# Second cross-attention of a decoder block: order of the matrix products in a window, place of the output projection, and the layout of its sums

## The chip, the cores and the metric
The kernel runs on one core of one Trainium2 chip. The metric is the time of one launch on the device, in microseconds (us). Three runs of the kernel before took 2831.57, 2815.93 and 2821.0 us; the median is 2821.0 us.

## What is computed
Six stages run one after the other on a tensor x of 4 batches x 512 tokens x 256 channels: attention, cross-attention and experts of layer 0, then linear attention, cross-attention and experts of layer 1. After each stage the result is added to x and normalised. The change is in the fifth stage and in the beginning of the sixth. The fifth computes

```
v = einsum('nlhd,ed->nlhe', context, Wv)      # 1024 context tokens, 16 heads of 16 channels
k = einsum('nlhd,ed->nlhe', context, Wk)
q = einsum('nlhd,ed->nlhe', x, Wq)            # 512 tokens of x
energy = einsum('nqhd,nkhd->nhqk', q, k)
attention = softmax(energy / sqrt(256), axis=-1)
out = einsum('nhql,nlhd->nqhd', attention, v).reshape(4, 512, 256)
x = layernorm(x + out @ Wo.T + bo)
```

The sixth sends every token through 16 experts and a shared one.

## The kernel before, in words
The function `l1_cross` (from L992) writes the stage. A unit is one batch with a group of four heads: 4 batches x 4 groups = 16 units, numbered 0 to 15. A unit has 8 windows, numbered 0 to 7, one for each block of 128 context tokens. The lists `between`, `after` and `at` (L1026 to L1039) name what each window does, and the function `side` gives that list to all five engines, each of which writes its own part of it, in that order. Nothing is scheduled afterwards.

In a window TensorE (PE) does the following for the current unit. The score products (`sc`, L1125) of two heads at a time write four banks of PSUM. They come in two halves: half 0 is heads 0 and 1, half 1 is heads 2 and 3. ScalarE (ACT) takes the exponential of a half (L1197). The value products (`pv`, L1110) of the block before follow; they use all 128 rows of the array.

Four more products in a window look ahead to the next unit (`max`, L1143). They are called maximum products 0, 1, 2 and 3 here. Each multiplies 128 queries of one head with 512 keys, and VectorE (DVE) takes the maximum of each row from PSUM (L1247), which the exponential needs later. Their heads are 2, 3, 0 and 1 (`max_of`), so that they stand on other rows of the array than the score products written beside them. After all 32 maxima of a unit, DVE merges them (`mq`, L1252), PE transposes them (`turn`, L1149), ACT copies them (L1217), and the DMA queue of SyncE (SP) writes them as a row under the queries (L1331).

Windows 0 to 4 of an even unit and 0 to 2 of an odd unit also carry a projection for the unit two ahead: `k` twice, `q`, and in even units `v` twice (L1155, L1159, L1166). These are called windows with a projection, the others windows without one. ACT evacuates `k` and `q` in two copies (L1205, L1207).

Maximum products, projections, `turn`, the output projection and transposes of x (`tp`) share three banks of PSUM in turn (`Turns`, `take`). Each may start only when the use three places before it in this ring has been read. The order of the ring in a window with a projection is: maximum products 0 and 1, projection, maximum products 2 and 3.

After the last block of a unit ACT copies the sums to `E` (`ev`, L1222). `E` holds in each group of 32 partitions 16 rows of values and 16 equal rows of the softmax's denominator. SP sends the denominators through DRAM (L1336, L1339), DVE inverts them (`rec`, L1256), SP writes them and reads them back broadcast (L1343, L1347), and GpSimd (POOL) multiplies (`mul`, L1307) into `OT`. `OT` has four slots of 128 partitions for a batch, half of whose rows carry nothing, and the weights `wo` have zeros there. When the four units of a batch are done, the output projection (`wo`, L1173) takes one product for each slot: four for each of the four tiles of 128 tokens. Then x is added (`res`), statistics are taken (`st`), x is scaled (`nr`) and transposed (`tp`). The last batch's output projection is done in the sixth stage (`l1_experts`, L2098).

Of the kernel before, what the change touches and what calls it, by code (L numbers as in the profile page):

```python
# [10 lines left out]
ALU = mybir.AluOpType  # L11
# [45 lines left out]
def program(nc, a, out):  # L57
    with ExitStack() as ctx:
# [89 lines left out]
        def dve_norm(dve, j, b, dst=None):  # L148
            dve.wait_ge(ln["ag"], 4 * j + 4)
            dve.wait_ge(ln["rstd"], j + 1)  # L150
            for i in range(4):
                t = 4 * b + i
                dve.e.tensor_scalar(x[:, t, :] if dst is None else dst(t), x[:, t, :], mv[:, i, 0:1], rstd[:, i:i + 1],
                                    ALU.subtract, ALU.mult).then_inc(ln["nrm"], 1)

# [836 lines left out]
        def l1_cross(c, wy, nx):  # L992
# [8 lines left out]
                                      "row0 row1 den0 den1 dc0 dc1 dr0 dr1 rb0 rb1 gsq gpow gs gtp gT xsq xpow rt lg sig chain")  # L1001
# [7 lines left out]
            R = [sbuf(c, "y_R0", [P, S]), nx["R"]]  # L1009
            OT = [sbuf(c, "y_OT0", [P, 4, S]), nx["OT"]]  # L1010
# [11 lines left out]
            def maxima(t):  # L1022
# [3 lines left out]
            between = {  # L1026
                0: [("pv", 0, 0), ("ev", -1, 0), ("k", 2, 0)],
                1: [("pv", 0, 1), ("k", 2, 1)],
                2: [("pv", 0, 2), ("q", 2, 0)],
                3: [("pv", 0, 3), ("v", 2, 0)],  # L1030
                4: [("pv", 0, 4), ("v", 2, 1)],
                5: [("pv", 0, 5)],
                6: [("pv", 0, 6), ("wo", -1, 0), ("res", -1, 0), ("wo", -1, 1)],
                7: [("pv", 0, 7), ("wo", -1, 2), ("res", -1, 2), ("wo", -1, 3)],
            }
            after = {0: [("st", -2, 0), ("xb", 0, 0)], 1: [("nr", -2, 0)], 2: [("tp", -2, 0)], 3: [("rec", -1, 0)], 4: [("tp", -2, 1)],
                     5: [("turn", 1, 0), ("mul", -1, 0)], 6: [("res", -1, 1)], 7: [("res", -1, 3)]}
            at = {t: [("sc", 0, 0), *maxima(t)[:2], *([("mq", 1, 0)] if t == 5 else []), *[w for w in between[t] if w[0] not in ("pv", "ev")],
                      ("sc", 0, 1), *maxima(t)[2:], *[w for w in between[t] if w[0] in ("pv", "ev")], *after[t]] for t in range(T)}  # L1039
# [8 lines left out]
            def side(u, t):  # L1048
                o = []
                for name, du, i in at[t]:  # L1050
                    v = u + du
                    if name == "pv" and 0 <= u * T + t - 1 < n * T:
                        o.append((name, u, t))
                        continue
                    if name == "sc" and 0 <= u < n and t < T:
                        o.append((name, u * T + t, i))
                        continue
                    once = name == "v" and v % 2 or name in ("pv", "sc")
# [5 lines left out]
                return o + (gate.get(t, []) if u == n - 1 else [])  # L1064
# [28 lines left out]
            def max_of(j):  # L1093

                return j // 8, j // 4 % 2, (2, 3, 0, 1)[j % 4]

# [31 lines left out]
            def pe_prog(pe):  # L1128
                begin(pe)
                for u, t in windows():  # L1130
                    gt = u * T + t
                    for name, v, j in side(u, t):
# [36 lines left out]
                        elif name == "wo":  # L1169
                            bank = take(pe, "wo", v, j)  # L1170
                            pe.wait_ge(s["mul"], v + 1)
                            for kk in range(4):
                                m = pe.e.matmul(bank[:, 0:D], OT[b % 2][:, kk, j * P:(j + 1) * P], wo[:, kk, :],  # L1173
                                                start=kk == 0, stop=kk == 3)
# [15 lines left out]
            def act_prog(act):  # L1190
                begin(act)
                for u, t in windows():
                    for name, v, j in side(u, t):
# [24 lines left out]
                        elif name == "ev":  # L1218
                            act.wait_ge(s["pv"], T * (v + 1))
                            act.wait_ge(s["mul"], v - 1)  # L1220
# [18 lines left out]
            def dve_prog(dve):  # L1239
                begin(dve)  # L1240
                for u, t in windows():
                    for name, v, j in side(u, t):
# [19 lines left out]
                        elif name == "st":  # L1262
                            dve.wait_ge(s["res"], 4 * (b + 1))
                            dve_stats(dve, 20 + b, b)
                        elif name == "nr":
                            dve_norm(dve, 20 + b, b)
# [10 lines left out]
            def pool_prog(pool):  # L1277
# [4 lines left out]
                for u, t in windows():  # L1282
                    for name, v, j in side(u, t):
# [19 lines left out]
                        elif name == "mul":  # L1303
                            pool.wait_ge(s[f"rb{v % 2}"], 16 * 4 * (v // 2 + 1))
                            pool.wait_ge(s["ev"], v + 1)
                            pool.wait_ge(s["ob"], 4 * (v // 4 - 1))
                            pool.e.tensor_tensor(OT[v // 4 % 2][:, v % 4, :], E[v % 2][:], R[v % 2][:], ALU.mult).then_inc(s["mul"], 1)  # L1307
                        elif name == "st":
                            pool_rstd(pool, 20 + v // 4)
                        elif name == "gw":  # L1310
                            pool.wait_ge(g["half"], 1)
                            pool.wait_ge(s["gsq"], 1)
                            pool.e.tensor_tensor(gn[:, 1:2], gn[:, 0:1], ex[0:NE, 1, 0:1], ALU.pow).then_inc(s["gpow"], 1)
                        elif name == "comb":
                            pool_gate(pool, s, 0, 12)

            def sp_prog(sp):
# [5 lines left out]
                for u, t in windows():  # L1323
                    for name, v, j in side(u, t):
# [8 lines left out]
                        elif name == "ev" and v < n - 1:  # L1333
                            sp.wait_ge(s["ev"], v + 1)
                            sp.wait_ge(s[f"dc{v % 2}"], 16 * (v // 2))
                            sp.e.dma_start(yd[v % 2], E[v % 2][16:P:32, :]).then_inc(s[f"den{v % 2}"], 16)  # L1336
                            sp.wait_ge(s[f"den{v % 2}"], 16 * (v // 2 + 1))
                            sp.wait_ge(s[f"dr{v % 2}"], 16 * (v // 2))
                            sp.e.dma_start(C[v % 2][:], yd[v % 2].rearrange("h (a n) -> (h a) n", n=16)).then_inc(s[f"dc{v % 2}"], 16)  # L1339
                        elif name == "rec":  # L1340
# [4 lines left out]
                            sp.wait_ge(s["mul"], v - 1)  # L1345
                            for h in range(4):
                                sp.e.dma_start(R[v % 2][32 * h:32 * h + 32, :], yr[v % 2][h].partition_broadcast(32)).then_inc(s[f"rb{v % 2}"], 16)  # L1347
# [694 lines left out]
        def l1_experts(c, wy, nx):  # L2042
# [8 lines left out]
            s = stage_sems(c, 5, "n", "xsq xpow rt lg sig chain den dc rec dr rb mul ob res wh wl xh xl up g h down acc o")  # L2051
# [12 lines left out]
            def pe_prog(pe):  # L2064
# [13 lines left out]
                for n, (e_, nb) in enumerate(steps):  # L2078
# [13 lines left out]
                    if n == 1:  # L2092
                        pe.wait_ge(s["mul"], 1)
                        for i in range(2):
                            for j in range(2):
                                qt = 2 * i + j
                                for kk in range(4):
                                    r = pe.e.matmul(A[i][:, j * D:(j + 1) * D], OT[:, kk, qt * P:(qt + 1) * P], wo[:, kk, :],  # L2098
                                                    start=kk == 0, stop=kk == 3)
# [97 lines left out]
            def pool_prog(pool):  # L2197
# [10 lines left out]
                pool.e.tensor_tensor(OT[:, 3, :], E[:], R[:], ALU.mult).then_inc(s["mul"], 1)  # L2208
# [7 lines left out]
            def sp_prog(sp):  # L2216
                begin(sp, True)
                sp.e.dma_start(yd[1], E[16:P:32, :]).then_inc(s["den"], 16)
                sp.wait_ge(s["den"], 16)
# [4 lines left out]
                for h in range(4):  # L2224
                    sp.e.dma_start(R[32 * h:32 * h + 32, :], yr[1][h].partition_broadcast(32)).then_inc(s["rb"], 16)
# [28 lines left out]
        with ExitStack() as c1:  # L2254
            wy = {n: sbuf(c1, f"y_{n}", sh) for n, sh in (("wo", [P, 4, D]), ("bo", [P, D]), ("wqk", [P, 2, 2, P]), ("wv", [P, P]), ("part", [P, 1]),
# [12 lines left out]
            for n, sh in (("E", [P, S]), ("C", [P, 16]), ("R", [P, S]), ("OT", [P, 4, S]), ("gw", [NE, D]), ("gn", [NE, 4]), ("gsq", [P, D]),  # L2268
# [43 lines left out]
def layouts(i):  # L2312
# [37 lines left out]
    wo = np.zeros((16, 32, D), np.float32)  # L2350
    wo[:, 0:16, :] = f("L1_xattn_Wo").T.reshape(16, 16, D)
    o["y_wo"] = kt(wo.reshape(512, D))
# [21 lines left out]
```

## Time and profile before

| | us |
|---|---|
| profiled execution, its time | 2816.93 |
| its span, first to last instruction | 2815.0 |
| median of three runs | 2821.0 |
| PE busy | 2569.0 (91% of the span) |
| DVE busy | 1468.7 (52%) |
| ACT busy | 1128.8 (40%) |
| POOL busy | 1086.5 (39%) |

The mean clock granted to TensorE is 0.952 of full speed. Times in rows are microseconds from the start of the span. A busy time is the union of what ran on an engine. `PEld` is the loading of weights, and `SPq` the DMA issues of SyncE. "x2" is the number of instructions merged in a row. `issue` is idle time for which the profile shows no cause. The part in brackets is the engine's idle time ahead of the row and what ended it. The fifth stage runs from about 1960 to 2470 us.

### The profile page before, as it was taken

How to read it: one execution, taken by the hardware profiler on the slowest of the kernel's cores; microseconds unless marked ns; L12 is line 12 of the kernel's file. 1: busy time of each engine (PE TensorE's matmuls, PEld its weight loads, DVE VectorE, ACT ScalarE, POOL GpSimd, SP SyncE). 2: the span in 40 equal slices, each digit the busy share in tenths (PEclk: the TensorE clock that was granted, in tenths of full speed). 3: DMA queues.
4: the chain of work that ended last, by engine and by line, in shares of the span. 5: the costliest groups of instructions: out<-in, count | busy, mean ns of one | idle time of the engine just before them, and what ended most of it. 6: DMA issues, size and time to landing. Idle time of an engine off the chain costs nothing.

```text
span 2815.0 us, 36748 instructions
## 1 busy us (share of the span) xinstructions
PE 2569.0 (91%) x13798; PEld 1529.8 (54%) x13798; DVE 1468.7 (52%) x3205; ACT 1128.8 (40%) x1614; POOL 1086.5 (39%) x735
## 2 busy tenths in 40 slices
PE   5786999999999999997999999687999999889997
PEld 3343556565556555654556665455333333368886
DVE  3444555555555555554433333366677777455455
ACT  3544344444444444442122222132576767631111
POOL 4665466666765676563100000142323323110001
PEclk8997999999999999997899999889799999999999
DMA  2001100000000000003899999510000000000000
GB/s 104 9 9 34 36 12 24 21 19 12 27 18 20 12 12 25 12 1 115 346 372 380 388 386 378 193 39 18 16 22 18 21 17 10 13 16 21 23 23 32
DMA packets 60322, 229.21 MB, mean 81 GB/s; under 512 B 16601, under 2 KB 30577, under 8 KB 44273
## 3 DMA queue, kind: packets, MB, share of 16 engines
q1 hardware_dynamic: 54256, 209.27, 20.2%
q0 software_dynamic: 3584, 9.84, 1.2%
q10 hardware_dynamic: 2304, 7.75, 0.7%
q8 instruction: 110, 1.80, 0.3%
q14 instruction: 68, 0.55, 0.1%
HBM read 216.73 MB, written 9.70 MB: 80 GB/s over the span
## 4 chain that ended last, share of the span: by engine, by line
PE 76%; DVE 9%; issue 4%; DMA 4%; ACT 3%; POOL 3%; SPq 1%; POOLq 0%; ACTq 0%; DVEq 0%
PE PS L680 8%; PE PS L1488 7%; PE PS L663 6%; PE PS L2087 6%; PE PS L711 5%; PE PS L721 4%; PE PS L1506 4%; PE PS L1110 4%; PE PS L2075 4%; PE PS L1125 3%; DMA m_fb<-in_m_fb 3%; PE PS L695 3%; PE PS L1143 3%; DVE y_Mx L1247 2%; PE PS L744 2%
## 5 line engine op out<-in xcount | busy, mean ns | idle before, releaser
L944 POOL TENSOR_TENSOR x_A<-x_A,x_P 128x1024 f32<-128x1024 f32 x190 | 451.4, 2376 | 203.1 <-ACT x_P L791 189.1
L871 DVE CUSTOM_DVE_ANT_0 x_junk<-PS,x_mb 128x512 bf16<-128x512 f32 x512 | 331.0, 685 | 352.2 <-PE PS L695 351.9
L1247 DVE TENSOR_REDUCE y_Mx<-PS 128x1 f32<-128x512 f32 x512 | 324.4, 685 | 126.6 <-PE PS L1143 126.6
L791 ACT ACTIVATE x_P<-PS,x_kb 128x1024 f32<-128x1024 f32 x256 | 271.8, 1112 | 222.8 <-PE PS L667 218.3
L1197 ACT ACTIVATE y_P<-PS 128x1024 f32<-128x1024 f32 x256 | 255.0, 1023 | 113.8 <-PE PS L1125 109.8
L1488 PE MATMUL PS<-m_w,m_xt 128*128 128x512 f32 x624 | 282.8, 596 | 0.6 <-issue 0.6
L680 PE MATMUL PS<-x_P,x_V 128*64 128x512 f32 x1024 | 248.8, 607 | 0.0
L663 PE MATMUL PS<-x_Q,x_K 64*128 64x512 f32 x1536 | 228.4, 400 | 0.0
L1143 PE MATMUL PS<-y_K,y_Q 16*128 16x512 f32 x512 | 188.2, 515 | 32.5 <-DVE y_Mx L1247 28.8
L2087 PE MATMUL PS<-n_xp,n_wp 128*128 128x512 f32 x816 | 211.8, 409 | 4.3 <-POOL n_wp L2203 4.3
L1709 POOL DMA_INDIRECT m_xb<-xd,m_idxi x39 | 37.1, 951 | 405.1 <-PE PS L1476 372.7
L1488 PEld LDWEIGHTS PS<-m_w,m_xt 128*128 128x128 f32 x624 | 116.3, 192 | 116.6 <-issue 114.7
L2087 PEld LDWEIGHTS PS<-n_xp,n_wp 128*128 128x128 f32 x816 | 155.2, 191 | 37.5 <-POOL n_wp L2203 6.0
L1125 PE MATMUL PS<-y_Q,y_K 32*128 32x512 f32 (+1 forms) x1024 | 162.1, 443 | 4.5 <-ACT y_P L1197 2.9
L663 PEld LDWEIGHTS PS<-x_Q,x_K 64*128 64x128 f32 x1536 | 141.1, 185 | 39.4 <-issue 11.3
L1689 DVE TENSOR_TENSOR m_gb<-PS,m_fb 128x1024 f32<-128x1024 f32 x39 | 47.8, 1225 | 198.5 <-DMA m_fb<-in_m_fb 117.0
L1506 PE MATMUL PS<-m_v,m_ht 128*128 128x256 f32 x624 | 141.8, 380 | 8.8 <-ACT m_ht L1572 8.8
L1125 PEld LDWEIGHTS PS<-y_Q,y_K 32*128 32x128 f32 (+1 forms) x1024 | 72.3, 190 | 141.1 <-issue 81.8
L1110 PE MATMUL PS<-y_P,y_V 128*32 128x512 f32 x1024 | 141.8, 628 | 0.0
L1506 PEld LDWEIGHTS PS<-m_v,m_ht 128*128 128x128 f32 x624 | 117.6, 190 | 44.0 <-issue 29.9
L2129 ACT ACTIVATE n_g<-PS 128x512 f32<-128x512 f32 x68 | 40.6, 597 | 250.3 <-PE PS L2087 250.3
L2075 PE MATMUL PS<-n_wd,n_h 128*128 128x256 f32 x544 | 130.0, 382 | 9.5 <-DVE x L2159 9.5
(333 smaller groups left out, 4239.8 us busy)
## 6 DMA issues: line engine op xcount, KB each, us to landing
m_w<-in_m_w SPq DMA_DIRECT2D x39, 2048.0 KB, 11.0
m_fb<-in_m_fb SPq DMA_DIRECT2D x39, 1024.0 KB, 12.9
m_v<-in_m_w SPq DMA_DIRECT2D x39, 1024.0 KB
x_w<-in_x_w SPq DMA_DIRECT2D x32, 384.0 KB, 3.0
ys<-m_yb SPq DMA_DIRECT2D x39, 128.0 KB
n_wg<-in_n_w SPq DMA_DIRECT2D x17, 256.0 KB, 2.8
x_cT<-in_ctxT SPq DMA_DIRECT2D x4, 1024.0 KB, 5.2
y_c<-in_ctxT SPq DMA_DIRECT2D x6, 512.0 KB, 3.7
```

Of the source, the lines that this page charges most:

```text
L663: pe.e.matmul(one_bank[2 * i + h], Ku[k][head(h), kt * P:(kt + 1) * P], Qu[q][head(h), :], start=first == 0, stop=False)
L680: m = pe.e.matmul(ob[head(h), :], V[v % 3][:, kt, head(h)], Pt[gt % 6][:, h, :], start=kt == 0, stop=kt == 7)
L791: act.e.activation(Pt[gt % 6][:], PS[:, 2 * i:2 * i + 2, :], ACT.Exp, bias=kb[u // 8 % 2][:, kt:kt + 1], scale=scale).then_inc(s["exp"], 1)
L871: dve.e.tensor_tensor_reduce(junk[j % 2][:], ring.bank("max", v, j), mb[b % 2][:, half * 512:half * 512 + 512], 1.0, -3e38, ALU.add, ALU.m ...
L944: pool.e.tensor_tensor(A[u % 2][:], Pt[(gt - 1) % 6][:] if kt == 1 else A[u % 2][:], Pt[gt % 6][:], ALU.add).then_inc(s["add"], 1)
L1125: m = pe.e.matmul(one_bank[h], Ku[i][r, t * P:(t + 1) * P], Qu[1 - i][r, :], start=i == 1, stop=i == 0)
L1143: pe.e.matmul(bank, Q[v % NBK][0][r, qt * P:(qt + 1) * P], K[v % NBK][0][r, half * 512:(half + 1) * 512], start=True, stop=True).then_inc( ...
L1197: act.e.activation(Pt[(2 * v + j) % 4][:], PS[:, 2 * j:2 * j + 2, :], ACT.Exp, scale=scale).then_inc(s["exp"], 1)
L1247: dve.e.tensor_reduce(Mx[v % 2][:, h, qt, half:half + 1], ring.bank("max", v, j), AX.X, ALU.max).then_inc(s["red"], 1)
L1488: r = pe.e.matmul(UP[si][:, half, :], XBT[j % 2][:, k, :], W1[j % 3][:, k, si, half * 512:half * 512 + 512], start=k == 0, stop=k == 1)
L1506: r = pe.e.matmul(Yb[:, 0:D], HT[j % 2][:, f, :], W2[j % 2][:, f, :], start=f == 0, stop=f == 7)
L2087: r = pe.e.matmul(bank[:, si, :], WP[e_ % 2][w][:, k, si, :], xp[xv][:, k, tok], start=k == 0 and j == 0, stop=k == 1 and j == 2)
```

## The change
Four things change; the arithmetic of every value that is kept is the same.

- The order in a window. `side` is rewritten: the score products of half 0, maximum products 0 and 1, the score products of half 1, then the projection, the value products, and after them maximum products 2 and 3. In a window without a projection maximum product 2 stands ahead of the value products and 3 behind them. `turn` stands where a projection stands, and the merge of the maxima is first in its window.
- The close of a batch. The output projection of a batch moves from windows 6 and 7 of the next unit (two tiles each) to windows 3, 4, 5 and 6 of the unit after it (one tile each). Statistics and scaling go tile by tile through the windows 4 to 7 and, a unit later, 1 to 4; the transposes stand in windows 4 and 6 of that unit.
- The sums. SP copies the 16 value rows of each head from `E` into dense rows of `OT` (four DMAs a unit). The broadcast writes 16 rows a head. POOL multiplies once for two units, in place. `OT` has two slots of 128 full rows, and each output tile takes two products.
- The sixth stage does the same for the last unit.

```diff
-            between = {
-                0: [("pv", 0, 0), ("ev", -1, 0), ("k", 2, 0)],
...
-                6: [("pv", 0, 6), ("wo", -1, 0), ("res", -1, 0), ("wo", -1, 1)],
-                7: [("pv", 0, 7), ("wo", -1, 2), ("res", -1, 2), ("wo", -1, 3)],
-            }
...
-            at = {t: [("sc", 0, 0), *maxima(t)[:2], *([("mq", 1, 0)] if t == 5 else []), *[w for w in between[t] if w[0] not in ("pv", "ev")],
-                      ("sc", 0, 1), *maxima(t)[2:], *[w for w in between[t] if w[0] in ("pv", "ev")], *after[t]] for t in range(T)}
+            beside = {0: [("k", 2, 0)], 1: [("k", 2, 1)], 2: [("q", 2, 0)], 3: [("v", 2, 0), ("wo", -2, 0), ("res", -2, 0)],
+                      4: [("v", 2, 1), ("wo", -2, 1), ("res", -2, 1)], 5: [("turn", 1, 0), ("wo", -2, 2), ("res", -2, 2)],
+                      6: [("wo", -2, 3), ("res", -2, 3)], 7: []}
+            behind = {0: [("ev", -1, 0), ("xb", 0, 0)], 1: [("nr", -3, 0)], 2: [("nr", -3, 1)], 3: [("rec", -1, 0), ("nr", -3, 2)],
+                      4: [("st", -2, 0), ("nr", -3, 3), ("tp", -3, 0)], 5: [("mul", -1, 0), ("st", -2, 1)],
+                      6: [("st", -2, 2), ("tp", -3, 1)], 7: [("st", -2, 3)]}
...
+                scores = [("sc", u * T + t, i) for i in range(2) if 0 <= u < n and t < T]
+                mx, mid = live(u, t, maxima(t)), live(u, t, beside[t])
+                pv = [("pv", u, t)] if 0 <= u * T + t - 1 < n * T else []
+                k = 2 if mid else 3
+                return [*live(u, t, [("mq", 1, 0)] if t == 5 else []), *scores[:1], *mx[:2], *scores[1:], *mx[2:k], *mid, *pv, *mx[k:],
+                        *live(u, t, behind[t]), *(gate.get(t, []) if u == n - 1 else [])]
...
+            def rows(v, h):
+                return slice(64 * (v % 2) + 16 * h, 64 * (v % 2) + 16 * h + 16)
...
-                            pe.wait_ge(s["mul"], v + 1)
-                            for kk in range(4):
+                            pe.wait_ge(s["mul"], 2 * (b + 1))
+                            for kk in range(2):
...
-                            pool.e.tensor_tensor(OT[v // 4 % 2][:, v % 4, :], E[v % 2][:], R[v % 2][:], ALU.mult).then_inc(s["mul"], 1)
+                            if v % 2:
+                                o = OT[v // 4 % 2][:, v // 2 % 2, :]
+                                pool.e.tensor_tensor(o, o, R[:], ALU.mult).then_inc(s["mul"], 1)
...
+                            sp.wait_ge(s["ob"], 4 * (v // 4 - 1))
+                            for h in range(4):
+                                sp.e.dma_start(OT[v // 4 % 2][rows(v, h), v // 2 % 2, :],
+                                               E[v % 2][32 * h:32 * h + 16, :]).then_inc(s[f"oc{v % 2}"], 16)
...
-                                sp.e.dma_start(R[v % 2][32 * h:32 * h + 32, :], yr[v % 2][h].partition_broadcast(32)).then_inc(s[f"rb{v % 2}"], 16)
+                                sp.e.dma_start(R[rows(v, h), :], yr[v % 2][h].partition_broadcast(16)).then_inc(s[f"rb{v % 2}"], 16)
```

On PE, in windows 1 and 2 of unit 4, two windows with a projection. L1125 is a half's score products, L1143 maximum products, L1155 and L1159 the projections of the keys' second half and of the queries, L1110 the value products. Before:

```order
L1125 MATMUL PS<-y_Q,y_K 128x512 x4
L1143 MATMUL PS<-y_K,y_Q 128x512 x2
L1155 MATMUL PS<-y_c,y_wqk 128x512
L1125 MATMUL PS<-y_Q,y_K 128x512 x4
L1143 MATMUL PS<-y_K,y_Q 128x512 x2
L1110 MATMUL PS<-y_P,y_V 32x512 x4
L1125 MATMUL PS<-y_Q,y_K 128x512 x4
L1143 MATMUL PS<-y_K,y_Q 128x512 x2
L1159 MATMUL PS<-xT,y_wqk 128x512
L1125 MATMUL PS<-y_Q,y_K 128x512 x4
L1143 MATMUL PS<-y_K,y_Q 128x512 x2
L1110 MATMUL PS<-y_P,y_V 32x512 x4
```

The same two windows now, where L1130, L1148, L1160, L1164 and L1115 are the same lines in turn:

```order
L1130 MATMUL PS<-y_Q,y_K 128x512 x4
L1148 MATMUL PS<-y_K,y_Q 128x512 x2
L1130 MATMUL PS<-y_Q,y_K 128x512 x4
L1160 MATMUL PS<-y_c,y_wqk 128x512
L1115 MATMUL PS<-y_P,y_V 32x512 x4
L1148 MATMUL PS<-y_K,y_Q 128x512 x2
L1130 MATMUL PS<-y_Q,y_K 128x512 x4
L1148 MATMUL PS<-y_K,y_Q 128x512 x2
L1130 MATMUL PS<-y_Q,y_K 128x512 x4
L1164 MATMUL PS<-xT,y_wqk 128x512
L1115 MATMUL PS<-y_P,y_V 32x512 x4
L1148 MATMUL PS<-y_K,y_Q 128x512 x2
```

Maximum products 2 and 3 moved from ahead of the value products to behind them, where only one half of score products stands between them and maximum products 0 and 1 of the next window. The projection moved behind the second half.

On PE, the close of batch 0. Before, window 6 of unit 4, with two tiles of the output projection (L1173) in one row:

```order
L1125 MATMUL PS<-y_Q,y_K 128x512 x4
L1143 MATMUL PS<-y_K,y_Q 128x512 x2
L1173 MATMUL PS<-y_wo,y_OT 128x256 x8
L1125 MATMUL PS<-y_Q,y_K 128x512 x4
L1143 MATMUL PS<-y_K,y_Q 128x512 x2
L1110 MATMUL PS<-y_P,y_V 32x512 x4
```

Now, from the middle of window 5 of unit 5 to the end of window 6 (L1154 is `turn`, L1178 a tile of the output projection):

```order
L1154 MATMUL PS<-ident,y_Mq 4x128 x4
L1178 MATMUL PS<-y_wo,y_OT 128x256 x2
L1115 MATMUL PS<-y_P,y_V 32x512 x4
L1148 MATMUL PS<-y_K,y_Q 128x512 x2
L1130 MATMUL PS<-y_Q,y_K 128x512 x4
L1148 MATMUL PS<-y_K,y_Q 128x512 x2
L1130 MATMUL PS<-y_Q,y_K 128x512 x4
L1178 MATMUL PS<-y_wo,y_OT 128x256 x2
L1115 MATMUL PS<-y_P,y_V 32x512 x4
L1148 MATMUL PS<-y_K,y_Q 128x512 x2
```

A tile has two products where it had four, and a window has one tile instead of two.

On SP, from the sums of one unit to the end of the denominators' way, before:

```order
L1336 DMA yd<-n_E 4x512
L1339 DMA n_C<-yd 128x16
L1343 DMA yr<-n_C 128x16
L1347 DMA n_R<-yr 32x512 x4
L1329 DMA y_K<-y_ones 4x1024
```

and the first three steps of it now:

```order
L1342 DMA yd<-n_E 4x512
L1345 DMA n_OT<-n_E 16x512 x4
L1349 DMA n_C<-yd 128x16
```

Four DMAs from SBUF to SBUF stand ahead of the load of the denominators.

## Rows read from the trace of the kernel before

**Rows 1.** Groups, 2005 to 2467 us: engine, operation, count; busy, mean ns; idle before.
```profile
L1143 PE MATMUL PS<-y_K,y_Q 16*128 16x512 f32 x460 | 160.7, 490 | 30.1 <-DVE y_Mx L1247 28.8
```

**Rows 2.** Timeline of unit 6, window 2, with a projection: start, duration, engine, line.
```profile
2181.48 0.50 PE L1125 MATMUL PS<-y_Q,y_K 32*128 32x512 f32 x2
2181.82 0.40 PE L1125 MATMUL PS<-y_Q,y_K 17*128 17x512 f32 x2
2182.14 1.12 PE L1159 MATMUL PS<-xT,y_wqk 128*128 128x512 f32 x2
2183.20 0.50 PE L1125 MATMUL PS<-y_Q,y_K 32*128 32x512 f32 x2
...
2183.80 0.59 ACT L1207 ACTIVATE y_F<-PS 128x512 f32<-128x512 f32 x1
2184.01 1.29 DVE L1247 TENSOR_REDUCE y_Mx<-PS 128x1 f32<-128x512 f32 x2 [0.43 <-PE PS L1143]
...
2184.06 1.06 PE L1110 MATMUL PS<-y_P,y_V 128*32 128x512 f32 x8
2184.28 1.03 ACT L1197 ACTIVATE y_P<-PS 128x1024 f32<-128x1024 f32 x1
...
2185.06 0.50 PE L1125 MATMUL PS<-y_Q,y_K 32*128 32x512 f32 x2
```

**Rows 3.** Timeline of unit 6, window 5, without a projection.
```profile
2192.23 0.50 PE L1143 MATMUL PS<-y_K,y_Q 16*128 16x512 f32 x2
...
2192.56 0.41 PE L1125 MATMUL PS<-y_Q,y_K 17*128 17x512 f32 x4
...
2192.81 0.40 PE L1125 MATMUL PS<-y_Q,y_K 17*128 17x512 f32 x2
...
2193.78 0.49 PE L1143 MATMUL PS<-y_K,y_Q 16*128 16x512 f32 x1 [0.57 <-DVE y_Mx L1247]
...
2194.20 1.06 PE L1110 MATMUL PS<-y_P,y_V 128*32 128x512 f32 x8
2194.24 0.18 DVE L1252 TENSOR_REDUCE y_Mq<-y_Mx 128x16 f32<-128x32 f32 x1
...
2195.20 0.60 PE L1149 MATMUL PS<-ident,y_Mq 128*4 128x128 f32 x4
...
2195.73 0.50 PE L1125 MATMUL PS<-y_Q,y_K 32*128 32x512 f32 x2
```

**Rows 4.** Timeline of ACT: the copies of the sums in units 3 to 7.
```profile
2086.35 0.61 ACT L1222 ACTIVATE y_E<-PS 128x512 f32<-128x512 f32 x1
...
2112.47 0.61 ACT L1222 ACTIVATE n_E<-PS 128x512 f32<-128x512 f32 x1
...
2148.02 0.62 ACT L1222 ACTIVATE y_E<-PS 128x512 f32<-128x512 f32 x1
...
2178.04 0.61 ACT L1222 ACTIVATE n_E<-PS 128x512 f32<-128x512 f32 x1
...
2205.39 0.60 ACT L1222 ACTIVATE y_E<-PS 128x512 f32<-128x512 f32 x1
```

**Rows 5.** Timeline of PE: two output tiles of batch 0, and what follows.
```profile
2131.88 3.69 PE L1173 MATMUL PS<-y_wo,y_OT 128*128 128x256 f32 x16 [0.99 <-POOL y_OT L1307]
...
2135.50 0.50 PE L1125 MATMUL PS<-y_Q,y_K 32*128 32x512 f32 x2
```

**Rows 6.** Timeline of SP: the issues of the broadcast of unit 5.
```profile
2190.70 1.71 SPq L1347 DMA_DIRECT2D n_R<-yr  x4
```

**Rows 7.** Stretches: busy time and count by engine, then PEclk, DMA share, GB/s.
```profile
2413.50:2431.00 17.50, 14.63 (x128) 5.27 (x124) 13.10 (x23) 12.06 (x13) 0.00 (x0) 1.00 0.08 17
1977.00:1995.00 18.00, 17.06 (x33) 7.52 (x32) 14.66 (x25) 4.04 (x6) 4.10 (x3) 0.50 0.10 30
```

**Rows 8.** Timeline of PE at unit 0, two starts of a window's first products.
```profile
2006.76 0.79 PE L1125 MATMUL PS<-y_Q,y_K 32*128 32x512 f32 x2
...
2012.54 0.50 PE L1125 MATMUL PS<-y_Q,y_K 32*128 32x512 f32 x2
```

More of the change, by code:

```diff
@@ L1046, in l1_cross, with live @@
                     3: [("squares", n - 1, 2)], 4: [("squares", n - 1, 3)], 5: [("comb", n - 1, 0)]}
-            def side(u, t):
+            def live(u, t, items):
                 o = []
-                for name, du, i in at[t]:
+                for name, du, i in items:
                     v = u + du
[L1052 to L1058, printed above, removed]
+                    once = name == "v" and v % 2
                     last = name in ("wo", "res", "st", "nr", "tp") and v % 4 != 3
@@ L1063, in side @@
                         o.append((name, v, i))
-                return o + (gate.get(t, []) if u == n - 1 else [])
+                return o
+            def side(u, t):
+                scores = [("sc", u * T + t, i) for i in range(2) if 0 <= u < n and t < T]
[4 more added lines that the diff above has]
+                        *live(u, t, behind[t]), *(gate.get(t, []) if u == n - 1 else [])]
             for u, t in windows():
@@ L2050, in l1_experts @@
             WP = [[sbuf(c, f"n_wp{i}{j}", [P, 2, 2, P], F32R) for j in range(2)] for i in range(2)]
-            s = stage_sems(c, 5, "n", "xsq xpow rt lg sig chain den dc rec dr rb mul ob res wh wl xh xl up g h down acc o")
+            s = stage_sems(c, 5, "n", "xsq xpow rt lg sig chain den oc dc rec dr rb mul ob res wh wl xh xl up g h down acc o")
             A, V2 = one_bank[0:2], one_bank[6:8]
@@ L2096, in pe_prog @@
                                 qt = 2 * i + j
-                                for kk in range(4):
+                                for kk in range(2):
                                     r = pe.e.matmul(A[i][:, j * D:(j + 1) * D], OT[:, kk, qt * P:(qt + 1) * P], wo[:, kk, :],
-                                                    start=kk == 0, stop=kk == 3)
+                                                    start=kk == 0, stop=kk == 1)
                             r.then_inc(s["ob"], 1)
@@ L2218, in sp_prog @@
                 sp.e.dma_start(yd[1], E[16:P:32, :]).then_inc(s["den"], 16)
+                for h in range(4):
+                    sp.e.dma_start(OT[64 + 16 * h:80 + 16 * h, 1, :], E[32 * h:32 * h + 16, :]).then_inc(s["oc"], 16)
                 sp.wait_ge(s["den"], 16)
@@ L2254, in program @@
         with ExitStack() as c1:
-            wy = {n: sbuf(c1, f"y_{n}", sh) for n, sh in (("wo", [P, 4, D]), ("bo", [P, D]), ("wqk", [P, 2, 2, P]), ("wv", [P, P]), ("part", [P, 1]),
+            wy = {n: sbuf(c1, f"y_{n}", sh) for n, sh in (("wo", [P, 2, D]), ("bo", [P, D]), ("wqk", [P, 2, 2, P]), ("wv", [P, P]), ("part", [P, 1]),
                                                          ("c0", [P, SX]), ("c1", [P, SX]))}
```

45 lines of the change are left out of this document (20 added, 25 removed).

## The prediction, made before the changed kernel was timed

> **What bounds the kernel now.** I read the page's busy shares first: PE is busy for 91% of the span, every other engine for about half or less (the table above). The fifth stage is no exception, and the grouped lines show that in it PE also waits 30.1 us ahead of maximum products, 28.8 of them for DVE's maxima [rows 1]. So the stage is a chain of PE's work and of waits for banks that DVE reads. The timelines of two windows then give every price.
>
> A window with a projection lasts 3.58 us (2181.48 to 2185.06). Its steps, start to start: score products of half 0 with maximum products beside them on other rows 0.66, projection 1.06, half 1 with maximum products 0.86, value products 1.00 [rows 2]. In half 0 the last score product starts at 2181.82 and the projection 0.32 later, which is how long that product holds the array.
>
> A window without a projection is ruled by a wait. Maximum product 0 starts at 2192.23, and product 3, which reuses its bank, at 2193.78, ended by DVE. So **from a maximum product's start to the reuse of its bank are 1.55 us**: the product, the signal, one maximum, the signal back. Value products start 0.42 after product 3, and take 1.00: 1.55 + 0.42 + 1.00 = 2.97 [rows 3]. DVE's two maxima take 1.29 together and one alone 0.68 (0.69), so the bank of a second product issued at once comes free about 0.61 later, at 2.16 [rows 2]. Two successive score products on the same rows start 0.33, then 0.25 apart (2192.23, 2192.56, 2192.81) [rows 3].
>
> **The change part by part.** Ring order is as before, so each maximum product 1 reuses the bank of product 2 of the window before, and a projection that of product 3. What changes is the work between these uses. Before, product 2 stood beside half 1, and the 1.00 of value products passed before product 1. Now products 2 and 3 stand behind the value products, and product 1 comes after a half of scores that needs only 0.58 (0.33 + 0.25). It must wait until 1.55, and PE takes its instructions in order, so half 1, the projection and the value products wait behind it, and behind those ACT's exponentials.
>
> Step 1, projection after projection. Count from the start of product 2 of the window before. Product 1 starts at 1.55. Half 1 has head 3 on product 1's rows: its first score product 0.33 later, its second 0.25 after that, and the array is free 0.32 later, 2.45. Product 3's bank is free at 2.16, so the projection starts at 2.45, and the next product 2 at 2.45 + 1.06 + 1.00 = 4.51. Against 3.58 that is **+0.93 a window**. Product 0 waits for ACT's second copy of the last projection. ACT's exponential of half 1 starts 0.22 after the array is free of it and takes 1.03 [rows 2], so it ends at 3.70; two copies like the row of 0.59 follow, to about 4.9, 0.4 of the next window. That is before 1.55 and adds nothing.
>
> Step 2, first window of a unit, after a window without projection. Only product 3 stands behind the value products; the projection waits for it: 1.55 + 1.06 + 1.00 = 3.61, +0.03. Step 3, window without projection after one with: product 2 waits for the second maximum, 2.16, then 0.42 + 1.00 = 3.58 against 2.97, +0.61. Step 4, without after without: product 2 waits for product 3 of the window before, 1.55 + 0.42 + 1.00 = 2.97: no change. Step 5, window 5 with `turn`: its transposes take 0.53 (2195.20 to 2195.73), and it lasted 0.53 + 2.97 = 3.50. In an even unit, after a projection: 2.45 + 0.53 + 1.00 = 3.98, +0.48. In an odd one the transposes wait for the last maximum and the merge (0.18 [rows 3], taken as 0.25 with its signals): 1.55 + 0.25 + 0.53 + 1.00 = 3.33, -0.17.
>
> Even units: 0.03 + 4 x 0.93 + 0.48 + 0.61 = 4.84. Odd units: 0.03 + 2 x 0.93 + 0.61 - 0.17 + 0.61 = 2.94. Units 0 to 13 project or prepare for later ones: 7 x 7.78 = **+54.5 us**.
>
> Step 6, the close of a batch. An odd unit lasts 26.12 (2086.35 to 2112.47), an even one 27.35 (2178.04 to 2205.39). From 2112.47 to 2148.02 and to 2178.04, where batch 0 closes, pass 35.55 and 30.02, so the close costs 65.57 - 53.47 = 12.1 us [rows 4], for three batches 36.3. Two tiles of the output projection last 3.62 [rows 5], a tile 1.81, and with two products instead of four 0.91. In windows 3, 4 and 6 a tile makes a window like one with a projection, 2.45 + 0.91 + 1.00 = 4.36, against 3.58, 2.97 and 3.58: 2.95. In window 5 the tile needs the bank of product 0, whose maximum is third on DVE behind the merge, about 3.0: 3.0 + 0.91 + 1.00 = 4.91 against 3.33, 1.58. Window 7 now follows a filled one: +0.61. Two sets of four transposes, priced like the four of `turn` (0.60 [rows 3]): 1.2. Together 6.3 a batch, 19.0 for three. **-17.3 us**. Statistics and scaling are the same work on DVE, which waits anyway in the longer windows; bounds 0 and the 12.1 a batch that the close costs now.
>
> Step 7, the sixth stage: four tiles, half the products: 4 x 0.91 = **-3.6 us**; PE has nothing else there, since its order is fixed.
>
> Step 8, the copies to dense rows. The trace has no such DMA; the nearest is the broadcast, four issues in 1.71 [rows 6]. If they held up the stage, 16 x 1.71 = 27 us; if not, 0. Behind them on SP stand the load of the denominators, then the broadcast and the row of maxima. The denominators are next read in window 3, three windows of over 3.5 later, so 1.7 fits in and I take 0. The sum of a batch is read by the output projection two units on. POOL's eight fewer multiplications hide under PE; 0 too.
>
> Sum: 2816.9 (the profiled execution's own time) + 54.5 - 17.3 - 3.6 = 2850.5. The median of the runs is 4.1 above that execution, so on its scale **2855 us**, 1.2% slower.
>
> **The clock.** Windows with 0.57 of idle each, one after another, kept the granted clock at 1.00 from 2413.5 to 2431; before the first unit, with PE busy 17.06 of 18.00 us, but with maximum products and projections only, it was 0.50 [rows 7]. These are the levels 2.4 and 1.2 GHz. The new windows wait up to 0.97 us (1.55 - 0.58) but keep all their scores and value products, so I take 2.4 GHz. The Trainium skill, "TensorE: Matmul & The Clock Gate", section "A second HAM failure mode: psum-queue depth-cycling", says that short idle gaps between groups of products that cycle through PSUM banks can make the clock swing between its levels. That rule speaks against this change. By it the sum would be that of rival C below. The trace does not bear it out for gaps of 0.57, and has no longer ones of this kind.
>
> **Rivals.** A: *the maxima come in time* (the other side). Place: maximum product 1. If the bank were free at 0.58 or sooner, not at 1.55, half 1 would run straight on: projection at 0.33 + 0.25 + 0.32 = 0.90, window 2.96, and DVE's four maxima (4 x 0.61 = 2.43) would rule windows without one. Eight windows a pair of units x -0.62, two with `turn` x -1.07, six x -0.54: -10.3 a pair, -72, with the close and the sixth stage -93: 2728. Against it stands the 1.55 itself, a measured row with no queue on DVE. Nothing but a shorter path than this row's would do it. 5%.
>
> B: *the waits replace others*. Half 0 already waits now and then for ACT, and if product 1's wait fell under such a wait, windows would keep their length and only -20.9 be left: 2800. For it: PE's 28.8 us of waits for DVE would move, not grow. Against: no row puts a wait of a microsecond between value products and half 1. 7%. A mixture, by which steps 1 and 3 cost a third of what I say, gives 2821 - 20.9 + 18 = 2818: 9%.
>
> C: *the clock falls.* Price: the window that began at 2006.76 with the clock at half lasted 5.78, 2.20 more than 3.58 [rows 8]. If a fourth of the 56 windows that carry a projection ran so, 14 x 2.2 = 31 us: 2886. For it: more idle in every window, and 18 us at 0.50 while PE looked busy [rows 7]. Against: the 1.00 of the first of these stretches. 8%.
>
> D: *the change does not save at the close* (tiles wait for the copies): 17 us back, 2872. 5%, with a range like my own.
>
> **How the numbers follow.** Forecast 66%, own range 2838 to 2872: each window's 0.93 may be 0.15 off, 56 x 0.15 = 8, and the close 8. With D 71%, C 8%, mixture 9%, B 7%, A 5%. What a measurement of this kernel can tell from no change is about 0.5%, 14 us: 2807 to 2835. Slower: 66 + 5 + 8 = 79%. Same: the mixture and a share of B, 10%. Faster: 11%. A range that leaves out A, B and part of C and reaches through the mixture's upper part is 2824 to 2886.
>
> **What would show it.** In the changed profile: windows with a projection at 4.5 us, those after them at 3.6, others 2.97; PE's idle ahead of maximum products tied to DVE at about 50 to 80 us instead of 28.8; DVE's idle longer by as much; output tiles of 0.9. Units of 29 (odd) and 32 us (even). Wrong would be: projection windows under 3.6, which makes A or B; a granted clock of 0.50 in the middle of the stage, which makes C; PE waiting for the products of POOL or for DMA of the dense rows, which makes D.

## The result, and the profile after

The changed kernel takes 2847.29 us (median of 4, 2840.4 to 2851.6) against 2820.68 before; the ratio is 1.0087, its 95% interval 1.0051 to 1.0122. It is slower by about 27 us, where 34 were forecast. The sign, the place and the mechanism hold. But two terms were wrong by 20 to 30 us each and went against each other, so that the total came near by luck. Without the one that the forecast left out, the clock, the corrected terms come to about 7 us, less than can be told from no change.

The grouped lines of the stage after, 2013 to 2505 us (engine, operation, count; busy, mean ns; idle before and its causes), answer to [rows 1]:

```profile
L1252 DVE TENSOR_REDUCE y_Mx<-PS 128x1 f32<-128x512 f32 x462 | 289.5, 682 | 144.5 <-PE PS L1148 143.9
L1148 PE MATMUL PS<-y_K,y_Q 16*128 16x512 f32 x462 | 153.0, 520 | 19.3 <-DVE y_Mx L1252 18.3
L1148 PEld LDWEIGHTS PS<-y_K,y_Q 16*128 16x128 f32 x462 | 61.7, 190 | 169.6 <-DVE y_Mx L1252 112.0 <-issue 54.7 <-ACT y_F L1212 1.4
```

The weight loads before, 2005 to 2467 us:

```profile
L1143 PEld LDWEIGHTS PS<-y_K,y_Q 16*128 16x128 f32 x460 | 62.1, 183 | 68.8 <-DVE y_Mx L1247 55.9 <-DVE x L1261 3.2 <-ACT y_NM L1217 2.2
```

PE's own idle ahead of maximum products fell, from 30.1 to 19.3, though the forecast was 50 to 80 for the part tied to DVE. The wait stands in the weight loads: 112.0 us for DVE, against 55.9 before. DVE's idle ahead of the maxima grew from 107.9 to 144.5. PE's row shows no idle time as long as any older product is still in the array, and the score products of half 0 cover a part of the wait.

A window with a projection after another one (unit 8, window 1), PE's timeline, answers to [rows 2]:

```profile
2270.11 0.49 PE L1148 MATMUL PS<-y_K,y_Q 16*128 16x512 f32 x1
2270.12 0.97 PE L1130 MATMUL PS<-y_Q,y_K 32*128 32x512 f32 x4
2271.02 1.12 PE L1160 MATMUL PS<-y_c,y_wqk 128*128 128x512 f32 x2
2272.07 1.06 PE L1115 MATMUL PS<-y_P,y_V 128*32 128x512 f32 x8
2273.07 0.74 PE L1148 MATMUL PS<-y_K,y_Q 16*128 16x512 f32 x3
...
2274.35 0.49 PE L1148 MATMUL PS<-y_K,y_Q 16*128 16x512 f32 x1 [0.31 <-DVE y_Mx L1252]
```

Maximum product 1 (2270.11), half 1, projection, value products, then products 2, 3 and 0 at 2273.07, and product 1 again at 2274.35. So the steps are the forecast's: 0.91 from product 1 to the projection (forecast 0.90), 1.05, 1.00. But from product 2 to product 1 it is 1.28 us, not 1.55. The window is 4.24, not 4.51. Windows without a projection (unit 8, windows 6 and 7) answer to [rows 3]:

```profile
2289.53 0.76 PE L1148 MATMUL PS<-y_K,y_Q 16*128 16x512 f32 x3
2289.87 0.63 PE L1130 MATMUL PS<-y_Q,y_K 32*128 32x512 f32 x4
2290.81 0.49 PE L1148 MATMUL PS<-y_K,y_Q 16*128 16x512 f32 x1 [0.31 <-DVE y_Mx L1252]
2290.81 0.95 PE L1130 MATMUL PS<-y_Q,y_K 32*128 32x512 f32 x4
2291.41 0.49 PE L1148 MATMUL PS<-y_K,y_Q 16*128 16x512 f32 x1
2291.83 1.06 PE L1115 MATMUL PS<-y_P,y_V 128*32 128x512 f32 x8
2292.83 0.49 PE L1148 MATMUL PS<-y_K,y_Q 16*128 16x512 f32 x1
...
2294.10 0.50 PE L1148 MATMUL PS<-y_K,y_Q 16*128 16x512 f32 x1
2294.53 1.07 PE L1115 MATMUL PS<-y_P,y_V 128*32 128x512 f32 x8
2295.53 0.49 PE L1148 MATMUL PS<-y_K,y_Q 16*128 16x512 f32 x1
```

Product 2 comes 1.88 after the products at 2289.53 (forecast 2.16), and value products 0.42 and product 3 1.00 later, as forecast. The next window, from product 3 to product 3, is 2.70 us where 2.97 had been forecast and measured: it got shorter.

ACT's copies of the sums answer to [rows 4] (units 6 to 8):

```profile
2210.83 0.60 ACT L1227 ACTIVATE n_E<-PS 128x512 f32<-128x512 f32 x1
...
2242.32 0.63 ACT L1227 ACTIVATE y_E<-PS 128x512 f32<-128x512 f32 x1
...
2269.34 0.63 ACT L1227 ACTIVATE n_E<-PS 128x512 f32<-128x512 f32 x1
```

An odd unit away from a close takes 27.0 (2242.32 to 2269.34) against 26.12, an even one 30.0 against 27.35 (the starts of units 7, 8 and 9 give 27.04 and 30.02). That is 3.6 us a pair, not 7.8.

The granted clock. Two stretches after (unit 0 begins at 2004), and one of before:

```profile
2004.00:2072.00 68.00, 68.00 (x247) 26.72 (x248) 28.43 (x47) 31.22 (x38) 15.85 (x11) 0.50 0.04 11
2073.00:2200.00 127.00, 120.32 (x788) 51.98 (x788) 89.64 (x156) 89.47 (x107) 32.61 (x23) 1.00 0.08 20
```
```profile
1996.00:2012.00 16.00, 15.99 (x58) 5.13 (x58) 7.48 (x13) 9.09 (x12) 8.71 (x6) 0.50 0.00 1
```

The clock was at half (1.2 GHz) when the stage's first scores came, in both kernels. In the kernel before it rose 16 us later, in the changed one 68 us later. PE's records are busy throughout in both. Units 0 and 1 take 82.8 us after and 59.5 before, 23.3 more, of which the waits at full clock explain 3.6.

Where the 34.8 us between the two profiled spans are, by the starts of units: ahead of unit 0, in stages that are not changed, +8.4; units 0 and 1 +23.4; units 2, 3, 7 and 11 +4.9; the nine units around the closes +1.4; unit 15 up to its last window +1.6; from there to the end, mostly the sixth stage, -5.0.

### The profile page after: what moved, and what is told of

Read it like the earlier page. It is cut to its first block, busy times and chain, and to the rows that moved or that the text cites. A ratio compares the mean times of both kernels' runs of the same rounds, so it can differ in the third digit from the quotient of the medians.

```text
span 2849.8 us, 36668 instructions
## 1 busy us (share of the span) xinstructions
PE 2620.2 (92%) x13734; PEld 1560.8 (55%) x13734; DVE 1460.9 (51%) x3205; ACT 1133.8 (40%) x1614; POOL 1075.7 (38%) x727
## 4 chain that ended last, share of the span: by engine, by line
PE 77%; DVE 8%; DMA 5%; issue 3%; ACT 3%; POOL 2%; SPq 1%; POOLq 0%; ACTq 0%; DVEq 0%
PE PS L686 8%; PE PS L2097 6%; PE PS L669 6%; PE PS L1498 5%; PE PS L717 5%; PE PS L1115 5%; PE PS L1148 5%; DMA m_fb<-in_m_fb 5%; PE PS L727 4%; PE PS L2085 4%; PE PS L1516 4%; PE PS L1130 3%; PE PS L701 3%; PE PS L750 2%; DVE y_Mx L1252 2%
## 5 line engine op out<-in xcount | busy, mean ns | idle before, releaser
L1130 PE MATMUL PS<-y_Q,y_K 32*128 32x512 f32 (+1 forms) x1024 | 204.3, 443 | 0.7 <-DMA y_Q<-y_NM 0.6
L1148 PE MATMUL PS<-y_K,y_Q 16*128 16x512 f32 x512 | 179.7, 541 | 21.7 <-DVE y_Mx L1252 18.3
L1148 PEld LDWEIGHTS PS<-y_K,y_Q 16*128 16x128 f32 x512 | 73.4, 197 | 189.9 <-DVE y_Mx L1252 126.4
L1115 PE MATMUL PS<-y_P,y_V 128*32 128x512 f32 x1024 | 150.4, 663 | 0.0
```

The lines of the kernel that those rows point to most:

```text
L1115: m = pe.e.matmul(ob[32 * h:32 * h + 32, :], V[v // 2 % 2][:, kt, v % 2 * 4 + h, :], Pt[(2 * gv + h // 2) % 4][:, h % 2, :], start=kt == 0 ...
L1130: m = pe.e.matmul(one_bank[h], Ku[i][r, t * P:(t + 1) * P], Qu[1 - i][r, :], start=i == 1, stop=i == 0)
L1148: pe.e.matmul(bank, Q[v % NBK][0][r, qt * P:(qt + 1) * P], K[v % NBK][0][r, half * 512:(half + 1) * 512], start=True, stop=True).then_inc( ...
```

## The experiments

Ratios are to the kernel before, on the same chip. The first four kernels below ran on one chip and the other four on a second one; the medians of the kernel before were 2825.57 us and 2826.21 us there. Differences to the changed kernel are to its 2847.29, which was taken apart from these, with 2820.68 for the kernel before, so they are good to some 5 us. Windows are start to start of half 0 unless something else is said. Times within the kernel are from one profile each.

**The old order with everything else new.** The order in `side`:

```diff
-                return [..., *scores[:1], *mx[:2], *scores[1:], *mx[2:k], *mid, *pv, *mx[k:],
+                return [..., *scores[:1], *mx[:2], *mid, *scores[1:], *mx[2:], *pv,
```

> The changed kernel with the window order of the kernel before (maximum products 2 and 3 beside half 1 and ahead of the value products, projection between the halves); late close, dense rows and the sixth stage as changed. Theory 1, the reused bank (maximum product 1 waits for the maximum of product 2 of the window before, and holds up all of PE behind it): windows go back to 3.58 and 2.97 us, the close keeps its gain and costs about 4 us a batch instead of 12, the sixth stage keeps its 3.6: about 2792 us, below both kernels. Theory 2, the copies to dense rows and the moved close are what costs, the order of a window costs nothing: stays at 2847.

Measured: 2789.44 us, ratio 0.9873 (0.984 to 0.9906). Windows 3.58 and 2.97, units 27.42 and 26.21, the two units of the first close 28.78 and 28.59. So the rest of the change saves 36 us, and the order costs 58 on top of it, its effect on the clock included. Theory 2 falls. Two starts of half 0 in unit 8, ahead of and behind a window with a projection, 3.58 apart:

```profile
2223.15 0.50 PE L1130 MATMUL PS<-y_Q,y_K 32*128 32x512 f32 x2
...
2226.73 0.50 PE L1130 MATMUL PS<-y_Q,y_K 32*128 32x512 f32 x2
```

**Only the new order.** In `side` of the kernel before, its list is sorted anew (a cut; `reorder` is a new function):

```diff
-                return o + (gate.get(t, []) if u == n - 1 else [])
+                return reorder(o) + (gate.get(t, []) if u == n - 1 else [])
```

> The kernel before with only the new order in a window; close of a batch, sparse rows and sixth stage as before. Theory 1: even units take 2.7 us more, odd ones 0.9, which is 25 us over units 0 to 13, and if the clock again stays at half through units 0 and 1, some 20 more: 2846 to 2866 us. Theory 2: 2821.

Measured: 2885.05 us, ratio 1.0193 (1.0155 to 1.0231), 19 us over the upper end of theory 1. Windows are 4.21 to 4.27, 2.96 and 2.70 as in the changed kernel; only windows 5 and 6 differ, since `turn` stays at the end of window 5. But the clock is low for 78.5 us around unit 0, and again after the closes for 27.3, 44.4 and 17.1 us: units 5, 9 and 13 take 39.4, 43.9 and 35.9, where the kernel before has 30.6, 31.9 and 31.9. That is more than the 19 us. The stretches around the first of these falls (unit 5 begins at 2170.7):

```profile
2160.00:2174.60 14.60, 12.12 (x70) 6.72 (x72) 6.67 (x12) 4.08 (x4) 0.00 (x0) 1.00 0.01 1
2174.60:2201.90 27.30, 27.30 (x103) 9.71 (x102) 14.70 (x32) 12.49 (x18) 8.22 (x7) 0.50 0.11 30
```

PE was idle for 2.5 of the 14.6 us ahead of the fall. No run here shows what brought the clock down.

**Unit 0 in the old order.**

```diff
+                if u < 1:
+                    return [..., *scores[:1], *mx[:2], *mid, *scores[1:], *mx[2:], *pv, ...]
```

> The changed kernel, but unit 0 and the units ahead of it keep the old order in a window. Theory 3, the longer waits keep the granted clock at half for the first two units: with denser windows in unit 0 the clock rises about 16 us into it, as before, and stays up; units 0 and 1 take 60 us instead of 83: about 2825 us. Theory 4, how long the clock stays low is chance and has nothing to do with the order: units 0 and 1 lose only the 3.5 us of their order, 2843 us, and the clock is as likely to be low until 2072 us as before.

Measured: 2821.55 us (10 runs), ratio 0.9987 (0.9965 to 1.0009), 26 below the changed kernel for an edit that alone shortens at most one unit's windows by 2.7 us. The stretches of its profile (unit 0 begins at 1999):

```profile
1999.00:2009.30 10.30, 10.29 (x34) 4.15 (x37) 5.80 (x10) 5.61 (x8) 5.08 (x3) 0.50 0.00 0
2009.30:2100.00 90.70, 86.07 (x579) 35.92 (x573) 63.80 (x107) 66.75 (x82) 26.13 (x20) 1.00 0.08 22
```

The clock rises 10 us into unit 0, and units 0 and 1 take 57.8 us. Units 1 to 8, in the new order with long waits, keep 1.00. Nor does this hang on one profile: the mean granted clock was 0.936 to 0.940 in the four runs of the changed kernel and 0.942 to 0.949 in these ten. Theory 3 holds against theory 4: in the changed kernel the order did not lower a clock that was up, it kept it from rising. The edit also puts back the order of the maximum products and projections ahead of unit 0, so no run tells whether it is unit 0 or what stands ahead of it. And with the clock's part gone the changed kernel cannot be told from the kernel before.

**Maximum products 0 and 1 ahead of half 0, in the kernel before.**

```diff
-            at = {t: [("sc", 0, 0), *maxima(t)[:2], ...
+            at = {t: [*maxima(t)[:2], ("sc", 0, 0), ...
```

> The kernel before with maximum products 0 and 1 issued ahead of half 0's score products instead of behind them. Theory 5, products stream in program order, so that a product recorded at 2192.23 really began about 0.26 later, behind the scores: from product 0 to the reuse of its bank are 1.28 us here, windows without a projection last 2.70 instead of 2.97, those with one about 3.38 instead of 3.58 since product 3 no longer waits: about 2797 us. Theory 6, the 1.55 us of the kernel before is the true way of a product's bank on those rows and the position beside scores does not matter: 2821.

Measured: 2812.72 us (12 runs), ratio 0.9957 (0.9938 to 0.9977). The timelines of PE and DVE in a window without a projection:

```profile
2189.24 0.50 PE L1143 MATMUL PS<-y_K,y_Q 16*128 16x512 f32 x2
...
2190.51 0.49 PE L1143 MATMUL PS<-y_K,y_Q 16*128 16x512 f32 x1 [0.32 <-DVE y_Mx L1247]
```
```profile
2189.77 2.48 DVE L1247 TENSOR_REDUCE y_Mx<-PS 128x1 f32<-128x512 f32 x4 [0.22 <-PE PS L1143]
```

From product 0's start to product 3's it is 1.27 us, where the same pair had 1.55 in [rows 3]. The maximum starts 0.53 after its product. In the window of [rows 3], in the kernel before, DVE's row was

```profile
2193.03 0.69 DVE L1247 TENSOR_REDUCE y_Mx<-PS 128x1 f32<-128x512 f32 x1 [0.54 <-PE PS L1143]
```

which is 0.80 after 2192.23. Windows are 2.70 and 3.39 (3.38 forecast), units 25.65 and 24.16. Theory 5 holds. Only 13 of the forecast 24 us arrive: windows 6 and 7 of the first close take 8.10 and 6.91 (7.01 and 6.57 before), the clock stays low for 51.2 us around unit 0 (44.4 before), and it is low for 10 us behind the second and the third close. The profile is of the fastest of the 12 runs, 2798.95 us; its mean clock is 0.946, and nine of the other eleven have 0.943 or less.

**Maximum product 1 behind half 1, in the changed kernel.**

```diff
-                return [..., *scores[:1], *mx[:2], *scores[1:], *mx[2:k], *mid, ...
+                return [..., *scores[:1], *mx[:1], *scores[1:], *mx[1:k], *mid, ...
```

> The changed kernel with maximum product 1 behind half 1's score products instead of ahead of them. Theory 1, the wait of product 1 costs because PE takes its instructions in order and half 1 stands behind it: half 1 now runs during the wait, the projection starts when product 3's bank is free (1.88 us after product 2 of the window before, with 1.28 from product to reuse) instead of 2.18: windows after windows with a projection 3.94 instead of 4.24, others as they are, about 2832 us by the median of 2847. Theory 7, it is the loss of company for products 2 and 3 (they stand alone on the array) and not the wait: 4.24 stays, 2847.

Measured: 2807.14 us, ratio 0.9934 (0.9911 to 0.9957). PE, from products 2 and 3 (2240.28) over half 0 and half 1, product 1 and the projection to the next products:

```profile
2240.28 0.74 PE L1148 MATMUL PS<-y_K,y_Q 16*128 16x512 f32 x3
2240.54 0.97 PE L1130 MATMUL PS<-y_Q,y_K 32*128 32x512 f32 x8
2241.56 0.49 PE L1148 MATMUL PS<-y_K,y_Q 16*128 16x512 f32 x1
2242.16 1.16 PE L1171 MATMUL PS<-y_wv,y_c 128*128 128x128 f32 x8
2243.25 1.06 PE L1115 MATMUL PS<-y_P,y_V 128*32 128x512 f32 x8
2244.24 0.52 PE L1148 MATMUL PS<-y_K,y_Q 16*128 16x512 f32 x3
```

From product 2 to product 2 it is 3.96, and the projection starts 1.88 after product 2, as theory 1 has it. (Start to start of half 0, windows 1 to 4 of this unit are 3.73 to 3.96, against 4.21 to 4.27.) Both halves run inside the wait. Of the 40 us below the changed kernel, units 2 to 14 give 16.0 in the profiles, near the forecast 15. Units 0 and 1 give 24.4, almost all of it the clock again: it rose early in unit 0 (at 2009), and they take 58.5 us.

**Maxima over half of the columns.** Half of the keys do not count in the maxima.

```diff
-                            ... ring.bank("max", v, j), AX.X,
+                            ... ring.bank("max", v, j)[:, 0:256], AX.X,
```

> The changed kernel with each maximum taken over 256 of its 512 columns, so that half of the keys do not count in the maxima; the number of instructions is the same. Theory 1, a maximum's duration is a term of each window: one takes 0.41 instead of 0.69, a second 0.33 instead of 0.61; product to reuse 1.00 instead of 1.28: 3.96 instead of 4.24 after a projection, 2.42 instead of 2.70 without one. Theory 7: 4.24 and 2.70 stay.

One run: 2791.18 us; a single time has no interval, and its windows are what is read here. Its maxima and one window, from products 2 and 3 to the next:

```profile
L1252 DVE TENSOR_REDUCE y_Mx<-PS 128x1 f32<-128x256 f32 x512 | 191.0, 418 | 232.8 <-PE PS L1148 228.9
```
```profile
2062.90 0.75 PE L1148 MATMUL PS<-y_K,y_Q 16*128 16x512 f32 x3
2063.24 0.64 PE L1130 MATMUL PS<-y_Q,y_K 32*128 32x512 f32 x4
2063.91 0.49 PE L1148 MATMUL PS<-y_K,y_Q 16*128 16x512 f32 x1
2063.91 0.95 PE L1130 MATMUL PS<-y_Q,y_K 32*128 32x512 f32 x4
2064.80 1.13 PE L1164 MATMUL PS<-xT,y_wqk 128*128 128x512 f32 x2
2065.85 1.07 PE L1115 MATMUL PS<-y_P,y_V 128*32 128x512 f32 x8
2066.85 0.74 PE L1148 MATMUL PS<-y_K,y_Q 16*128 16x512 f32 x3
```

Product to reuse 1.01, the window 3.95, windows without a projection 2.42: DVE's 0.26 us shorter maximum (682 to 418 ns) shortens each of the windows by about as much, 0.29 and 0.28, although DVE is busy for only 69% of units 2 to 14 in the changed kernel. PE's products are the same, so theory 7 falls.

**The late close alone.** The kernel before with the new lists `beside` and `behind`, statistics and scaling by tiles, in the old order:

```diff
-                6: [("pv", 0, 6), ("wo", -1, 0), ("res", -1, 0), ("wo", -1, 1)],
+            beside = {..., 3: [("v", 2, 0), ("wo", -2, 0), ("res", -2, 0)], ...
```

> The kernel before with only the close of a batch moved to the unit after and done tile by tile (turn and merge of the maxima moved with it); sparse rows, four products a tile, old order, old sixth stage. Of the 36 us that the old order with late close and dense rows is below the kernel before, the dense rows should have 12 x 0.91 + 3.6 = 14.5. Theory 9, the rest is the place of the close: 2825.6 - 21 = 2804 us. Theory 10, the place is worth nothing and the rest is something else: 2821 or more.

Measured: 2803.66 us, ratio 0.9907 (0.9877 to 0.9937). The place of the close is worth 22 us. What the old-order kernel is below this one, 14.2, is near the 14.5 reckoned for the dense rows; the two ratios, with some 8 us of interval each, put it at 10, so that the match is not closer than that. A tile here and one in the old-order kernel, each with what follows it:

```profile
2153.71 1.99 PE L1174 MATMUL PS<-y_wo,y_OT 128*128 128x256 f32 x8
2155.64 0.50 PE L1126 MATMUL PS<-y_Q,y_K 32*128 32x512 f32 x2
```
```profile
2151.86 1.13 PE L1178 MATMUL PS<-y_wo,y_OT 128*128 128x256 f32 x4
2152.93 0.50 PE L1130 MATMUL PS<-y_Q,y_K 32*128 32x512 f32 x2
```

A tile takes 1.93 with four products and 1.07 with two.

**The version that beats both.** The old order with maximum products 0 and 1 ahead of half 0, and the rest of the change:

```diff
-                return [..., *scores[:1], *mx[:2], *scores[1:], *mx[2:k], *mid, *pv, *mx[k:],
+                return [..., *mx[:2], *scores[:1], *mid, *scores[1:], *mx[2:], *pv,
```

> The old order in a window with maximum products 0 and 1 ahead of half 0, and the late close, the dense rows and the sixth stage of the changed kernel. Theory 5: windows 3.39 and 2.70 as with the early maximum products alone, units 1.8 us shorter than 27.42 and 26.21, close as with the old order: 2768 us. Theory 8, the less dense first units keep the clock low for longer and eat a part: 2775 to 2785.

Measured: 2769.78 us, ratio 0.9795 (0.9773 to 0.9818), 56 us below the kernel before and 77.5 below the changed one. Windows 3.39 and 2.70, units 25.7 and 24.2, as theory 5 has them; the median is near its 2768. Theory 8's clock is there too, in a profile of the slowest of the five runs, 2779.39 us: low for 58 us around unit 0, against 44.4 with the old order. So there may be something left.

## Why the prediction was right, and where it was not

**The mechanism (steps 1 and 3) is shown.** Product 1 waits for the maximum of product 2, and half 1 behind it waits too: moving product 1 behind half 1 took 0.28 us off the way from product 2 to product 2, shortening the maximum took 0.29 off, and undoing the order brought the windows back to 3.58 and 2.97. Of the 58 us that this gave, by the profiles about 25 are the windows, 20 the clock, and 11 that the close costs 3.7 us a batch in the old order and 7.4 in the new.

**The term of 1.55 was mis-sized, and with it steps 1 to 5.** It is 1.28. I read it from a product recorded at 2192.23 that stood behind four score products in PE's order. Its record begins before the last two of these (2192.56), and DVE's maximum starts 0.27 us later after it than after a product with no scores ahead of it. That is what one would see if the product streamed only behind the scores; the record itself does not show it. With the products ahead of the scores 0.27 us of the 1.55 are gone, and in the new order product 2 follows the value products with nothing in between. The Trainium skill, "TensorE: Matmul & The Clock Gate", section "Step-by-step: what each phase is for", has the rule: only weight loads are pulled ahead, products keep program order. The traces agree by the start of DVE's maximum, 0.80 after the record against 0.53. With 1.28 a window after a projection is 1.28 + 0.90 + 2.06 = 4.24, one without after one without 2.70; both are what was measured. Step 4, put at no change, is thus a gain of 0.27. Steps 1 to 5 with 1.28, and 1.88 for the second bank, give 2.67 for an even unit and 0.76 for an odd one, where 2.67 and 0.92 were measured: so this one term accounts for nearly the whole error of the windows. Their sum is 7 x 3.6 = 25 us instead of 54.5: 29 too much. That is less than half of the forecast, nearer to the mixture's third.

**Step 6**: the close cost 7.4 us a batch in the first (units 4 to 6: 94.4 against 87.0 for three others), forecast 6.3; by this batch the three save 14 us, not 17.3. **Step 7**: the four tiles take 3.26 us in the sixth stage (2523.96 to 2527.22) against 6.83 (2485.66 to 2492.49), the forecast 3.6 saved. The wait of 1.61 for POOL ahead of them is gone too, which was not forecast:

```profile
2485.66 7.17 PE L2098 MATMUL PS<-y_wo,n_OT 128*128 128x256 f32 x32 [1.61 <-POOL n_OT L2208]
```

**Step 8**: four copies take 2.43 on SP, nearest row 1.71, and no engine waits for them: 0, as taken. SP's rows after, with the next steps of that path:

```profile
2270.57 2.43 SPq L1345 DMA_DIRECT2D n_OT<-n_E  x4
2273.04 0.58 SPq L1349 DMA_DIRECT2D n_C<-yd  x1
2283.56 0.34 SPq L1353 DMA_DIRECT2D yr<-n_C  x1
```

**The clock was put at no cost and cost about 20 us.** I had looked at whether the new windows would lower it, by a stretch in which it was up. It starts the stage low, and the question was how soon it rises. Rival C had a price of 31 but the wrong place, and a chance of 8% was too small. The Trainium skill, "TensorE: Matmul & The Clock Gate", section "A second HAM failure mode: psum-queue depth-cycling", tells of a swing between the levels, set off by short idle gaps. In the middle of this stage the traces hardly show it: from unit 2 to unit 14 the changed kernel, with its waits in every window, was at half for one stretch of 3.4 us, and the kernel before for two. The kernel with the new order alone, which has the tiles of the close in pairs, was at half for 92 us there, in four stretches.

So 2855 came out near 2847 because 29 us too many in the windows met 20 too few in the clock. That is luck. With every term as measured the sum is 25 - 14 - 4 + 20 = 27 us, which is the difference found; the clock makes most of it, and without it the forecast "slower" would not have come true. With unit 0 in the old order it did not: ratio 0.9987. Rivals A and B fall: windows after a projection did get longer. D falls with step 8.

The medians of the kernel before lie up to 5 us apart, within its own scatter (2815.2 to 2839.1 in 23 runs). The 8.4 us ahead of unit 0 are scatter of this kind too: unit 0 begins between 1989 and 2005 us in the ten profiles, though nothing ahead of this stage is changed in any.

## What to carry to other kernels

When banks are shared in a ring, write for each use how much other work lies between it and the use before it, and compare that with product, signal, read, signal; moving a product away from the score products can turn a covered round trip into a stop for everything behind it on an engine that keeps its order. Put products that feed another engine ahead of those that don't: it was worth 0.27 us in a window without a projection here, and 0.19 in one with it. And before pricing a wait by a stretch at full clock, look at what the clock is when the stretch begins. A total that comes out near proves little; hold each term against its own row.

## What the runs showed of the hardware

- From a product's record to the start of its reader on DVE were 0.80 us where four score products on other rows stood ahead of it, and 0.53 where none did. So a bank's round trip read from such a record can be 0.27 us too long; the start of the reader tells.
- From a maximum product to the reuse of its bank were 1.28 us with a maximum over 512 columns (0.68 long) and 1.01 with one over 256 (0.42 long).
- With the clock low at the start of the stage, how long it stayed low went with the order of the first unit in every profile: 37.5 to 44.4 us with the old order there (four kernels), 37.6 with product 1 behind half 1, 51 to 58 with the products ahead of half 0, 58 with half maxima, 78.5 and 95.6 with the new order. From the start of unit 0 until the rise PE is busy for over 99% in all of them, so busy time does not tell them apart, and the cause stays open. These are single profiles; for the changed kernel and the one with unit 0 in the old order the medians (2847 and 2822) and the mean clocks say the same.
